# A graph network on one core: who makes the decay weights, who prunes and sums part of each cosine block, and how column sums are turned

## The chip, the cores and the metric

The kernel runs on one core of one Trainium2 chip. The metric is the device time of one execution in microseconds, median of three runs. Engines: TensorE (PE, with its weight loads PEld), VectorE (DVE), ScalarE (ACT), GpSimd (POOL), and SyncE (SP), whose queue issues all loads.

## The reference

The input is x (3327 x 64) and adj (3327 x 3327, about 0.5% non-zero and a full diagonal). Four layers each end in a layer norm of x plus the layer's output.

```python
# layer 0, twice:  x = tanh(concat([adj @ x, x]) @ W[k])
# layer 1:         1 - 0.1 * x - 0.01 * sum(x * (adj @ x), axis=1)
# layer 2:         support = x @ weight; mask = adj != 0; rank = cumsum(mask, axis=1)
#                  w = mask * (pos > 0) * 0.5 ** (k - pos)     # the last 100 neighbours
#                  w @ support + bias
# layer 3, for it in range(2), H = adj:
Q = x @ Wq + bq;  V = x @ Wv + bv;  edge_feat = H.T @ V
att = softmax(Q @ edge_feat.T * scale * H, axis=1);  att_scores = att.mean(axis=0)
comp_mask = softmax(0.5 * structural + 0.5 * att_scores) >= th_comp
cos = xn @ xn.T                                   # of the masked, normalised rows
edge_scores = softmax(cos * H, axis=1)
H_pruned = H * ((edge_scores >= th_edge) & comp_mask[:, None])
connectivity = H_pruned.sum(axis=1)               # row sums; the column sums are edeg
node_mask = softmax(connectivity * feat_mag) >= th_node, where connected
agg = (H_pruned.T * dv_isqrt) @ (x_final @ W) / edeg
x = relu(dv_isqrt * (H_pruned @ agg) @ Theta)
```

## The kernel before

adj is padded to 3328 x 3328 and cut into 26 blocks of 128 rows (1664 KB each in float32). Each stage streams the blocks again; SyncE issues their loads in order, each after a wait for the slot that it overwrites (`block_done`).

The stages, with their times in the profile: two hops and the ODE layer (to 279 us), the decay layer (to about 473), and then twice edge, attention, cosine, down and up (edge 474 to 553, attention 554 to 677, cosine 688 to 900, down and up 904 to 1108; the second iteration ends the kernel).

The decay layer makes, for 26 blocks in two column halves (q = 0, 1), 52 steps. In each, TensorE counts neighbours in PSUM with triangular matrices (`own_bits`, `rest_tri`), ScalarE (`L1015`) and VectorE (`L1270`) turn the counts of two partition halves into bf16 weights with a relu into int16, one half each, in chunks of 512 and 320 columns, and TensorE multiplies them with the support, which was split in three bf16 parts (`split_part`, L1201, starting with a scaling by 2**27, L1206). VectorE also makes the next block's mask (L1254). In the first steps the layer norm of the ODE layer is still under way: it is done in three parts of the nodes (2, then 1, then 0), with `drift_part` (L1191), `centre_part` (L1143), `square_part` and `root_part` on ScalarE, `var_part`, `scale_part`, and then TensorE's turn of x (`early_turn`, L664) and `support_part` (L671). Their places in both queues are written out by step number.

The attention and cosine passes are alike: TensorE makes a block of products in four pieces of 832 columns, VectorE multiplies each with adj and takes the row maximum (`product_piece`, L1317), then the maximum over the pieces (L1328); ScalarE takes the exponential in place with its row sum (L1069). In the cosine pass VectorE then makes the row's cut (`cut_of`, L1439); ScalarE writes the sign of cut minus exponential for the later stages (L1087) and VectorE prunes the block in its slot in one instruction with its row sum (`prune`, L1447), one block behind the pieces. Two product buffers (`prod`) are used in turn. TensorE adds up the columns of the pruned slot two blocks behind (`columns`, L766), which frees the slot; there are four slots.

After each of these passes a row of column sums is copied to SBUF and turned into node order by TensorE (`turn_sums`, L811), in the attention pass ahead of the node softmax, in the cosine pass among the down stage's first blocks. A node softmax has its maximum and sum over partitions on GpSimd (L528, L530), which has nothing else to do after its memsets. `keep_running` puts matmuls with zeros (512 columns) into TensorE's queue.

In down and up the slots are pruned by the stored signs (L1475, L1489) before TensorE gathers.

## Time and profile before

| | |
|---|---|
| median of 3 runs | 1776.97 us (1773.96 to 1777.36) |
| the profiled execution | 1778.09 us, its span 1776.3 us |
| mean granted TensorE clock | 0.954 |
| TensorE busy | 1536.9 us, 87% |
| VectorE busy | 1192.9 us, 67% |
| ScalarE busy | 683.8 us, 38% |
| GpSimd busy | 4.0 us, 17 instructions |
| chain that ended last | PE 50%, DVE 26%, DMA 20%, ACT 2% |
| HBM over the span | 325 GB/s |

The span is what the profiler sees of one execution; the device time is 1.8 us more. Shares are means over all stages. The chain is followed back from the last instruction, at each step to what released it.

### The profile page before, as it was taken

Reading aid. Unit: us, or ns where it says so; the run is one execution under the profiler, and the core shown is the slowest. Engines: PE = TensorE matmul, PEld = TensorE weight load, DVE = VectorE, ACT = ScalarE, POOL = GpSimd, SP = SyncE. Lnnn points to the kernel's source line nnn. Section 1 sums busy time; section 2 is a strip of 40 time slices with the busy share of each in tenths; the row PEclk is TensorE's granted clock in tenths of the full one; section 3 lists DMA queues with packets and bytes.
Section 4 is the critical chain, followed back from the end, with each engine's and each line's share of the span. In section 5 each row is a group of like instructions: output and inputs, shape, how many; then the busy total and the mean of one; then the engine's idle time right before and its main releaser. Section 6 shows DMA issues by size and latency. Waiting matters only on the chain.

```text
span 1776.3 us, 22361 instructions
## 1 busy us (share of the span) xinstructions
PE 1536.9 (87%) x9521; PEld 617.7 (35%) x9549; DVE 1192.9 (67%) x1668; ACT 683.8 (38%) x520; POOL 4.0 (0%) x17
## 2 busy tenths in 40 slices
PE   6789998899999997777787799999997777797895
PEld 2234433334433333222232344443333222232442
DVE  0000306777505996999989798117977999989897
ACT  0000101333213665787720242015665777700441
POOL 0000000000000000000000000000000000000000
PEclk9999999999999999888889999999998888799998
DMA  9979596799799993656579999999992566599993
GB/s 404 427 283 426 231 426 233 245 341 410 304 426 392 394 378 123 221 206 228 193 297 427 420 421 425 426 426 406 381 370 77 196 228 219 179 389 425 426 426 166
DMA packets 60611, 578.29 MB, mean 326 GB/s; under 512 B 6240, under 2 KB 6496, under 8 KB 20832
## 3 DMA queue, kind: packets, MB, share of 16 engines
q1 hardware_dynamic: 60512, 576.87, 81.1%
q8 instruction: 75, 1.23, 0.3%
q14 instruction: 24, 0.20, 0.0%
HBM read 575.14 MB, written 1.70 MB: 325 GB/s over the span
## 4 chain that ended last, share of the span: by engine, by line
PE 50%; DVE 26%; DMA 20%; ACT 2%; issue 2%; SPq 0%; DVEq 0%; POOL 0%; ACTq 0%
PE ps L545 48%; DMA slot<-adj 10%; DVE pairs L1317 10%; DMA arena<-adj_t 7%; DVE slot L1447 7%; DVE slot L1475 3%; DMA slot<-adj_t 2%; PE ps L895 2%; DMA x_kept<-cur 1%; DVE slot L1489 1%; ACT pairs L1069 1%; DVE pairs L1270 1%; DVE hats L1489 0%; DVE hats L1475 0%; DVE pairs L1475 0%
## 5 line engine op out<-in xcount | busy, mean ns | idle before, releaser
L1317 DVE CUSTOM_DVE_ANT_1 pairs<-ps,slot 128x832 f32<-128x832 f32 x352 | 342.6, 1020 | 30.1 <-PE ps L545 14.9
L1069 ACT ACTIVATE pairs<-pairs,negmax 128x3327 f32<-128x3327 f32 x88 | 270.0, 3069 | 135.1 <-DVE negmax L1328 135.1
L545 PE MATMUL ps<-hats 64*128 64x416 f32 x832 | 225.8, 651 | 101.9 <-DVE max L1317 100.7
L545 PE MATMUL ps<-slot,cur 128*64 128x512 f32 (+1 forms) x1536 | 281.1, 515 | 28.7 <-DVE slot L1475 16.2
L545 PE MATMUL ps<-arena 64*128 64x416 f32 (+1 forms) x1072 | 207.6, 524 | 2.2 <-DVE max L1317 1.6
L1447 DVE SCALAR_TENSOR_TENSOR slot<-pairs,cut,slot 128x3327 f32<-128x3327 f32 x52 | 191.1, 3676 | 0.1
L545 PEld LDWEIGHTS ps<-slot,cur 128*64 128x64 f32 x1536 | 103.4, 137 | 202.3 <-issue 163.3
L1087 ACT ACTIVATE arena<-pairs,cut 128x3328 fp8e4<-128x3328 f32 x52 | 159.7, 3072 | 26.3 <-DVE cut L1439 26.3
L545 PEld LDWEIGHTS ps<-hats 64*128 64x128 f32 x832 | 77.8, 216 | 241.1 <-DVE max L1317 194.5
L1137 DVE COPY pairs<-ps 128x512 f32<-128x512 f32 x3 | 2.1, 692 | 195.0 <-PE ps L545 195.0
L545 PEld LDWEIGHTS ps<-arena 64*128 64x128 f32 (+1 forms) x1072 | 87.6, 175 | 122.4 <-DVE max L1317 64.1
L1106 ACT ACTIVATE hats<-ps 128x2048 int16<-128x2048 int16 (+1 forms) x28 | 42.1, 1554 | 227.0 <-PE ps L895 226.9
L545 PE MATMUL ps<-slot,ones 128*32 128x416 f32 x832 | 100.3, 608 | 7.1 <-DVE slot L1447 7.1
L1475 DVE SCALAR_TENSOR_TENSOR slot<-arena,slot 128x3328 f32<-128x3328 int8 x28 | 100.7, 3622 | 6.0 <-DMA slot<-adj 5.9
L545 PE MATMUL ps<-pairs,arena 128*64 128x512 bf16 (+2 forms) x736 | 94.8, 372 | 1.0 <-DMA pairs<-adj 1.0
L545 PE MATMUL ps<-pairs,hats 128*128 128x512 bf16 (+1 forms) x392 | 86.0, 339 | 9.3 <-DVE pairs L1270 6.1
L545 PE MATMUL ps<-slot,arena 128*64 128x512 f32 x480 | 87.8, 515 | 3.3 <-DMA slot<-adj 3.3
L1015 ACT ACTIVATE pairs<-ps 128x512 int16<-128x512 f32 x104 | 53.0, 517 | 92.5 <-PE ps L545 88.2
L1270 DVE TENSOR_SCALAR pairs<-ps 128x512 int16<-128x512 f32 x104 | 60.6, 590 | 37.4 <-PE ps L545 33.1
L948 ACT ACTIVATE pairs<-ps 128x640 f32<-128x640 f32 (+1 forms) x6 | 3.9, 650 | 198.4 <-PE ps L545 198.4
L1489 DVE SCALAR_TENSOR_TENSOR slot<-hats,slot 128x3328 f32<-128x3328 int8 x20 | 72.0, 3620 | 8.6 <-ACT hats L1106 6.4
L545 PE MATMUL ps<-arena,cur 128*64 128x512 f32 (+1 forms) x384 | 68.6, 513 | 1.0 <-DMA arena<-adj_t 1.0
(178 smaller groups left out, 1453.7 us busy)
## 6 DMA issues: line engine op xcount, KB each, us to landing
slot<-adj SPq DMA_DIRECT2D x162, 1664.0 KB, 9.2
slot<-adj_t SPq DMA_DIRECT2D x64, 1664.0 KB, 15.1
arena<-adj_t SPq DMA_DIRECT2D x26, 1664.0 KB, 23.4
arena<-adj_t SPq DMA_DIRECT2D x52, 832.0 KB, 6.5
arena<-adj SPq DMA_DIRECT2D x15, 1664.0 KB, 14.8
pairs<-adj SPq DMA_DIRECT2D x15, 1664.0 KB, 15.6
pairs<-adj_t SPq DMA_DIRECT2D x12, 1664.0 KB, 14.4
hats<-adj SPq DMA_DIRECT2D x8, 1664.0 KB, 12.5
```

The source lines that it names most:

```text
L545: return pe.matmul(o, l, r, start=start, stop=stop, skip_group_check=True)
L895: last = pe.transpose(ps[:, 4 * BANK + q * D:4 * BANK + (q + 1) * D].bitcast(BF16), sign_pairs[:, q * HALF + pair * P:q * HALF + (pair + 1 ...
L948: act.activation(agg_f[:, CHUNK_COLS[c]], ps[:, CHUNK_COLS[c]], ACT.Copy).then_inc(early_cols[c], 1)
L1015: act.activation(dst, bank(c, w), ACT.Relu).then_inc(relu_act, 1)
L1069: act.activation(bufs[b][:, 0:N], bufs[b][:, 0:N], ACT.Exp, bias=negmax[:, b:b + 1], accum_out=rowsum[:, b:b + 1]).then_inc(exp_done, 1)
L1087: act.activation(interleaved(sign_marks[:, row * NP:(row + 1) * NP]), halves(prod[k % 2][:, 0:NP]), ACT.Sign, bias=cut[:, k % 2:k % 2 + 1] ...
L1106: act.activation(turned[pair % 2][:, cols], ps[:, 4 * BANK:4 * BANK + HALF].bitcast(I16)[:, cols], ACT.Copy)\
L1270: dve.tensor_scalar(dst, bank(2 + c, w), 0.0, None, ALU.max).then_inc(relu_dve, 1)
L1317: dve.tensor_tensor_reduce(out=pieces3(bufs[k % len(bufs)], c), in0=pieces_psum(piece_place(name, k, c)[0]), in1=pieces3(slot_of(name, k), ...
L1447: dve.scalar_tensor_tensor(out=slot[:, 0:N], in0=prod[k % 2][:, 0:N], scalar=cut[:, k % 2:k % 2 + 1], in1=slot[:, 0:N], op0=ALU.is_ge, op1 ...
L1475: dve.scalar_tensor_tensor(out=slot, in0=interleaved(signs[:, row * NP:(row + 1) * NP]), scalar=0.0, in1=slot, op0=ALU.is_le, op1=ALU.mult ...
L1489: dve.scalar_tensor_tensor(out=slot, in0=interleaved(turned[k // 2 % 2].bitcast(I8))[:, k % 2], scalar=0.0, in1=slot, op0=ALU.is_le, op1=A ...
```

## The change

In the decay layer ScalarE makes both halves' weights in the first ten steps (`ACT_STEPS`). The weight of the support is scaled by 2**27 once at the start, and the split reads PSUM itself. A part's drift is centred through its row sums: a reduce over the whole of `scr_a` is done ahead, the mean then follows from small operations. Part 1's drift comes behind the split of part 2, ScalarE's square, turn and copy of the parts move by a step.

After an attention pass eight fillers stand ahead of the last block's column sums and three instead of six behind; eight instead of twelve follow the turn. The turn is thirteen transposes and a matmul into two banks; VectorE reads the result with four instructions instead of one.

In the cosine passes the last 512 columns of blocks 0 to 23 are pruned by GpSimd (a comparison into `share_marks`, then a product in the slot), and summed by ScalarE, which copies them into `share_sink` with a row sum, one block behind, after the next block's exponential and sign. VectorE prunes the other columns and adds the sums of both. The column sums, the reuse of `prod` and the slots' reloads wait for the new steps. Behind its last share GpSimd makes a reduction of ones over the partitions that nobody reads.

```diff
+ACT_STEPS = 10
+def weights_made(q, k, c):
+    n = 2 * (q * NB + k) + c + 1
+    return n + min(n, 2 * ACT_STEPS), max(0, n - 2 * ACT_STEPS)
...
+SHARE = 512
+SHARED = NB - 2
...
+        def turned_sums(t):
+            at = 4 * BANK + t * P if t < MID else 6 * BANK + (t - MID) * P if t < 2 * MID else 4 * BANK + MID * P
+            return ps[:, at:at + P]
...
+                    behind = free - 1 - BASE[f"cos{it}"]
+                    if kind in ("cos", "down") and 0 <= behind < SHARED:
+                        sp.wait_ge(share_summed, it * SHARED + behind + 1)
...
+            def prune_share(it, k):
+                slot = slot_of(f"cos{it}", k)
+                cols = slice(N - SHARE, N)
+                pool.wait_ge(row_cut, it * NB + k + 1)
+                if it * SHARED + k:
+                    pool.wait_ge(share_pruned, it * SHARED + k)
+                pool.tensor_scalar(share_marks[:, :], prod[k % 2][:, cols], cut[:, k % 2:k % 2 + 1], None, ALU.is_ge)\
+                    .then_inc(share_marked, 1)
+                pool.wait_ge(share_marked, it * SHARED + k + 1)
+                pool.tensor_tensor(slot[:, cols], slot[:, cols], share_marks[:, :], ALU.mult).then_inc(share_pruned, 1)
...
             for it in range(2):
                 node_softmax(2 * it)
+                for k in range(SHARED):
+                    prune_share(it, k)
+                pool.partition_all_reduce(tiny["unused"][:, :], ones32[:, 0:1], P, RADD).then_inc(reduction_loaded, 1)
                 node_softmax(2 * it + 1)
...
+            pe.wait_ge(consts_made, 5)
+            pe.wait_ge(consts_cast, 4)
             support_part(2)
-            pe.wait_ge(consts_made, 5)
-            pe.wait_ge(consts_cast, 3)
             for q in range(2):
                 if q:
-                    pe.wait_ge(relu_act, 2 * NB)
-                    pe.wait_ge(relu_dve, 2 * NB)
+                    by_act, by_dve = weights_made(0, NB - 1, 1)
+                    pe.wait_ge(relu_act, by_act)
+                    pe.wait_ge(relu_dve, by_dve)
...
-                        pe.wait_ge(relu_act, 2 * (q * NB + k) + c + 1)
-                        pe.wait_ge(relu_dve, 2 * (q * NB + k) + c + 1)
+                        by_act, by_dve = weights_made(q, k, c)
+                        pe.wait_ge(relu_act, by_act)
+                        if by_dve:
+                            pe.wait_ge(relu_dve, by_dve)
...
+                        if k < SHARED:
+                            pe.wait_ge(share_pruned, it * SHARED + k + 1)
...
                 columns(NB - 2)
+                pe.wait_ge(piece_read, (g + 1) * NB * 4 + 5)
+                keep_running(8 if sums else 0)
                 columns(NB - 1)
-                pe.wait_ge(piece_read, (g + 1) * NB * 4 + 5)
                 mm(bank(5, 1), zeros_b[:, :], ones_b[:, 0:1]).then_inc(colsum_psum, 1)
-                keep_running(6)
+                keep_running(3 if sums else 6)
...
-                whole, split = ident[:, 0:P:D], ident[:, 32:P:D]
-                for t in range(MID):
-                    mm(turned_sums[:, 2 * t:2 * t + 2], col_rows[:, t * P:(t + 1) * P], whole)
-                    b = MID + 1 + t
-                    mm(turned_sums[:, 2 * b:2 * b + 2], col_rows[:, D + t * P:D + (t + 1) * P], split)
-                middle = turned_sums[:, 2 * MID:2 * MID + 2]
-                mm(middle[0:D], col_rows[:, MID * P:MID * P + D], whole)
-                mm(middle[D:P], col_rows[:, 0:D], split).then_inc(colsum_t, 1)
+                for t in range(2 * MID):
+                    o = t * P + t // MID * (P // 2 - MID * P)
+                    pe.transpose(turned_sums(t), col_rows[:, o:o + P], ident)
+                pe.transpose(turned_sums(2 * MID)[0:D], col_rows[:, MID * P:MID * P + D], ident)
+                mm(turned_sums(2 * MID)[D:P], col_rows[:, 0:D], ident).then_inc(colsum_t, 1)
...
-                keep_running(12)
+                keep_running(8)
...
-            square_part(4, 1)
...
+                        if q * NB + k < ACT_STEPS:
+                            act.wait_ge(tri_done, 4 * (q * NB + k) + 2 * c + 2)
+                            dst = decay[k % 2].bitcast(I16)[:, QUART + o:QUART + o + w]
+                            act.activation(dst, bank(2 + c, w), ACT.Relu).then_inc(relu_act, 1)
                     if q == 0 and k == 0:
+                        square_part(4, 1)
                         root_part(4, 1)
-                    elif q == 0 and k == 1:
+                    elif q == 0 and k == 2:
                         early_xt(1)
-                    elif q == 0 and k == 2:
                         square_part(5, 0)
                     elif q == 0 and k == 4:
                         root_part(5, 0)
-                    elif q == 0 and k == 5:
+                    elif q == 0 and k == 6:
...
+                def sum_share(k):
+                    at = place(ROW_ORDER["cos"][k])
+                    act.wait_ge(share_pruned, it * SHARED + k + 1)
+                    if it * SHARED + k:
+                        act.wait_ge(share_summed, it * SHARED + k)
+                    act.activation(share_sink[:, :], slot_of(f"cos{it}", k)[:, N - SHARE:N], ACT.Copy,
+                                   accum_out=small["conn_share"][:, at:at + 1]).then_inc(share_summed, 1)
                 for k in range(NB):
                     exp_and_sign(k)
+                    if 0 < k <= SHARED:
+                        sum_share(k - 1)
...
+            def drift_product(c):
+                dve.wait_ge(folded, 6 + 3 - c)
+                link(dve.tensor_tensor(of_part(scr_b, c), blocks3(early_psum(c)), of_part(cur[:, :], c), ALU.mult))
             def drift_part(c):
-                dve.wait_ge(folded, 6 + 3 - c)
                 mean = part_small(small["mean"][:, :], c)
-                link(dve.tensor_tensor(of_part(scr_b, c), blocks3(early_psum(c)), of_part(cur[:, :], c), ALU.mult))
                 link(dve.tensor_reduce(mean, of_part(scr_b, c), axis=X, op=ALU.add))
-                link(dve.tensor_scalar(mean, mean, 0.01, None, ALU.mult))
-                link(dve.tensor_tensor(of_part(scr_a, c), of_part(scr_a, c), part_spread(small["mean"][:, :], c),
-                                       ALU.subtract))
+                drift = part_small(small["dv"][:, :], c)
+                link(dve.tensor_scalar(drift, mean, 0.01, None, ALU.mult))
+                link(dve.scalar_tensor_tensor(out=mean, in0=part_small(small["rnorm"][:, :], c), scalar=1.0 / D, in1=drift,
+                                              op0=ALU.mult, op1=ALU.subtract))
+                link(dve.tensor_tensor(mean, mean, drift, ALU.add))
+                dve.tensor_tensor(of_part(scr_a, c), of_part(scr_a, c), part_spread(small["mean"][:, :], c),
+                                  ALU.subtract).then_inc(part_centred, 1)
...
-                link(dve.tensor_scalar(part, blocks3(early_psum(c)), float(1 << DECAY_SHIFT), None, ALU.mult))
-                link(dve.tensor_copy(sup[:, :, 0], part))
-                link(dve.tensor_tensor(part, part, sup[:, :, 0], ALU.subtract))
+                link(dve.tensor_copy(sup[:, :, 0], blocks3(early_psum(c))))
+                link(dve.tensor_tensor(part, blocks3(early_psum(c)), sup[:, :, 0], ALU.subtract))
...
+            dve.tensor_scalar(W["decay_w"], W["decay_w"], float(1 << DECAY_SHIFT), None, ALU.mult).then_inc(consts_cast, 1)
...
+            link(dve.tensor_reduce(small["rnorm"][:, :], blocks3(scr_a), axis=X, op=ALU.add))
             early_evac(2, "ode")
+            drift_product(2)
             drift_part(2)
-            centre_part(2)
-            drift_part(1)
+            drift_product(1)
             var_part(3, 2)
             ready_part(3, 2)
-            centre_part(1)
...
             split_part(2)
+            drift_part(1)
             for q in range(2):
                 if q:
                     mask_of(0, q)
                     mask_of(1, q)
                 for k in range(NB):
-                    dve.wait_ge(decay_used, q * NB + k + 3)
-                    for c, (o, w) in enumerate(QUART_CHUNKS):
+                    for c, (o, w) in enumerate(QUART_CHUNKS if q * NB + k >= ACT_STEPS else ()):
+                        if c == 0:
+                            dve.wait_ge(decay_used, q * NB + k + 3)
...
+                        drift_product(0)
                         drift_part(0)
-                    elif q == 0 and k == 2:
-                        centre_part(0)
...
+                            dve.wait_ge(share_marked, g // 2 * SHARED + min(k - 1, SHARED))
...
+            def on_column_sums(g, use):
+                dve.wait_ge(colsum_t, g + 1)
+                def pairs_of(t, part, rows):
+                    v = t[rows, 2 * part * (MID + 1):2 * part * (MID + 1) + 2 * MID]
+                    return v.rearrange("p (b h) -> p b h", h=2)
+                everything = slice(0, P)
+                for part in range(2):
+                    v = ps[:, (4 + 2 * part) * BANK:(4 + 2 * part) * BANK + MID * P]
+                    v = v.rearrange("p (b h r z) -> p b h r z", h=2, r=2, z=32)[:, :, :, part, 0]
+                    use(v, lambda t, part=part: pairs_of(t, part, everything))
+                    rows = slice(part * D, part * D + D)
+                    v = turned_sums(2 * MID)[rows].rearrange("p (h r z) -> p h r z", h=2, r=2)[:, :, part, 0]
+                    last = use(v, lambda t, rows=rows: t[rows, 2 * MID:2 * MID + 2])
+                return last
...
-                dve.wait_ge(colsum_t, 2 * it + 1)
-                link(dve.scalar_tensor_tensor(out=S["node_z"], in0=turned_sums, scalar=0.5 / N, in1=S["imp"],
-                                              op0=ALU.mult, op1=ALU.add))
+                def score(sums, of):
+                    return dve.scalar_tensor_tensor(out=of(S["node_z"]), in0=sums, scalar=0.5 / N, in1=of(S["imp"]),
+                                                    op0=ALU.mult, op1=ALU.add)
+                link(on_column_sums(2 * it, score))
...
-                    dve.scalar_tensor_tensor(out=slot[:, 0:N], in0=prod[k % 2][:, 0:N],
-                                             scalar=cut[:, k % 2:k % 2 + 1], in1=slot[:, 0:N], op0=ALU.is_ge,
+                    cols = slice(0, N - SHARE if k < SHARED else N)
+                    dve.scalar_tensor_tensor(out=slot[:, cols], in0=prod[k % 2][:, cols],
+                                             scalar=cut[:, k % 2:k % 2 + 1], in1=slot[:, cols], op0=ALU.is_ge,
                                              op1=ALU.mult, accum_out=S["conn"][:, at:at + 1]).then_inc(pruned, 1)
...
+                dve.wait_ge(share_summed, (it + 1) * SHARED)
+                link(dve.tensor_tensor(S["conn"], S["conn"], S["conn_share"], ALU.add))
...
-                        dve.wait_ge(colsum_t, 2 * it + 2)
-                        dve.tensor_scalar(S["edeg"], turned_sums, 1e-6, None, ALU.max).then_inc(edeg_read, 1)
+                        on_column_sums(2 * it + 1, lambda sums, of: dve.tensor_scalar(
+                            of(S["edeg"]), sums, 1e-6, None, ALU.max)).then_inc(edeg_read, 1)
```

## Rows read from the trace of the kernel before

**Rows 1.** Windows: length; busy PE, PEld, DVE, ACT, POOL; PE clock, DMA share, GB/s.
```profile
440.00:450.00 10.00, 9.84 (x67) 3.82 (x68) 7.50 (x11) 3.60 (x7) 0.00 (x0) 1.00 1.02 412
450.00:460.00 10.00, 9.84 (x71) 3.94 (x70) 6.02 (x10) 3.52 (x8) 0.00 (x0) 1.00 0.24 91
680.00:900.00 220.00, 163.47 (x888) 55.28 (x891) 203.99 (x322) 162.36 (x80) 0.74 (x2) 0.85 0.50 180
900.00:1000.00 100.00, 85.36 (x492) 33.48 (x490) 83.73 (x37) 5.93 (x8) 0.74 (x2) 0.98 0.97 403
```

**Rows 2.** Timeline of a cosine block: start, duration, instruction, [idle before].
```profile
714.37 0.16 DVE L1328 TENSOR_REDUCE negmax<-max 128x1 f32<-128x4 f32 x1
714.45 3.67 DVE L1447 SCALAR_TENSOR_TENSOR slot<-pairs,cut,slot 128x3327 f32<-128x3327 f32 x1
717.54 0.19 ACT L1069 ACTIVATION_READ_ACCUMULATOR pairs<-pairs,negmax 128x1 f32 x1
718.05 0.15 DVE L1439 SCALAR_TENSOR_TENSOR cut<-rowsum,blocked 128x1 f32<-128x1 f32 x1
718.37 1.02 DVE L1317 CUSTOM_DVE_ANT_1 pairs<-ps,slot 128x832 f32<-128x832 f32 x1 [0.17 <-DVE slot L1447]
722.27 0.16 DVE L1328 TENSOR_REDUCE negmax<-max 128x1 f32<-128x4 f32 x1
722.46 3.07 ACT L1069 ACTIVATE pairs<-pairs,negmax 128x3327 f32<-128x3327 f32 x1 [1.15 <-DVE negmax L1328]
```

**Rows 3.** Timeline where the cut of block 1 waits for the exponential.
```profile
702.09 0.19 ACT L1069 ACTIVATION_READ_ACCUMULATOR pairs<-pairs,negmax 128x1 f32 x1
702.31 0.16 DVE L1439 SCALAR_TENSOR_TENSOR cut<-rowsum,blocked 128x1 f32<-128x1 f32 x1 [2.46 <-ACT pairs L1069]
```

**Rows 4.** Timeline of GpSimd's memset at the start and its first reduction.
```profile
0.86 0.53 POOL L520 MEMSET ones_b<- 128x512 bf16 x1
...
683.06 0.18 DVE L1357 TENSOR_REDUCE pmax<-node_z 128x1 f32<-128x26 f32 x1
683.33 0.35 POOL L528 PARTITION_ALL_REDUCE gmax<-pmax  x1 [681.71 <-DVE pmax L1357]
```

**Rows 5.** First cosine pass: waits (total, times, longest), and the chain (start, length).
```profile
DVE pairs L1317 <- DMA slot<-adj: 3.9, 4, 1.9
...
814.38 8.65 DMA slot<-adj
```

**Rows 6.** Timeline of the decay stage's start; last, its row of waits.
```profile
279.99 0.82 DVE L1195 TENSOR_TENSOR arena<-ps,cur 128x640 f32<-128x640 f32 x1 [0.79 <-PE ps L660]
286.94 0.82 DVE L1152 TENSOR_REDUCE mean<-arena 128x10 f32<-128x640 f32 x1
289.26 1.33 PE L668 MATMUL ps<-cst,cur 128*128 128x128 f32 x5 [3.26 <-DVE cur L1159]
294.46 0.83 DVE L1206 TENSOR_SCALAR arena<-ps 128x640 f32<-128x640 f32 x1 [1.86 <-PE ps L545]
...
298.81 1.02 PE L545 MATMUL ps<-pairs,hats 128*128 128x512 bf16 x4
334.73 1.04 PE L545 MATMUL ps<-pairs,hats 128*128 128x512 bf16 x4
337.64 1.04 PE L545 MATMUL ps<-pairs,hats 128*128 128x512 bf16 x4
...
PE ps L545 <- DVE pairs L1270: 6.1, 15, 1.0
```

**Rows 7.** Groups by form, 300 to 400 us: ScalarE's weights of a decay step.
```profile
L1015 ACT ACTIVATE pairs<-ps 128x512 int16<-128x512 f32 x31 | 18.5, 595 | 29.9 <-PE ps L545 27.8 <-remote 2.1
L1015 ACT ACTIVATE pairs<-ps 128x320 int16<-128x320 f32 x31 | 13.5, 437 | 21.0 <-PE ps L545 21.0
```

**Rows 8.** Timeline: turning the column sums, and thirteen transposes elsewhere.
```profile
679.84 2.95 PE L545 MATMUL ps<-cst,pairs 128*128 128x2 f32 x28
...
279.18 1.64 PE L660 MATMUL ps<-cst,pairs 128*128 128x128 f32 x13
```

12 lines of the change are left out of this document (9 added, 3 removed).

## The prediction

> **What bounds the kernel now.** I read busy time by stage first, then the chain that ended last, then the instructions in order of time where the change touches them. TensorE's share over the whole span misleads, as the stages differ [rows 1]. In the decay stage (300 to 450 us) TensorE is the limit: busy 9.84 of 10 us. In the down stage the DMA queues are full, at 403 GB/s, and up and the next edge stage are like it. In the cosine pass (680 to 900, and a second one like it in iteration 1) VectorE is busy 204 of 220 us, DMA half the time, and TensorE waits, at a mean clock of 0.85. A gain in a cosine pass is kept, since the DMA-bound stretch behind it starts when the pass is over; a gain inside a DMA-bound stretch is lost.
>
> The cosine pass in order of time [rows 2]. Per block VectorE does four pieces (P), the maximum (M), the pruning of the block before (R, 3.67) and the cut (C); ScalarE does the exponential (E), then the sign (S). From M at 714.37: R, then C at 718.05 (3.68 later), P at 718.37, next M at 722.27: a period of 7.90 us. E, its accumulator read included, is over at 717.73, M+3.36. R is the later of the two, but only by 0.3 us. ScalarE idles 1.15 us ahead of the next E, so S ended at M+6.94.
>
> **The cosine prune.** R loses 512 of 3327 columns: at 3.67/3327 per column 0.57 us. C then waits for E instead. How fast C follows E is shown where it waits for it already: E's accumulator read ends at 702.28, C starts at 702.31 [rows 3]. So C comes at M+3.39 instead of M+3.68, and the period becomes 7.61: of 0.57 us 0.29 is paid out. It counts for blocks 2 to 24, 23 per pass, since C(1) waits for E already and R of the last two blocks stays whole: 6.7 us per pass.
>
> ScalarE gets a copy of 512 columns with a sum. Nearest rows: an activation of 128x512 in the decay stage, 0.595 [rows 7], and 0.19 for the read of an accumulator [rows 2]: 0.8 us, between S(k) and E(k+1). S would end at M+6.65, the copy at M+7.45, E(k+1) may start at M+7.80. It fits, with some 0.35 us left. A copy of over 1.15 us would begin to eat the gain; at 1.45 it is gone. Slot reloads now wait for this sum too, but the column sums of the same block on TensorE end after M(k+2), and this sum before it, so that costs nothing.
>
> GpSimd gets two operations of 512 columns per block, from C(k) on. The trace shows none of the kind. Nearest row: its memset of 128x512, 0.53 [rows 4], one stream. A stream for each operand read and for the result makes 2 + 3 of them, 2.65 us: my value. Two memsets, 1.1 us, are the low end, twice the value, 5.3 us, the high end. VectorE's next R starts 4.2 us after C (0.32 to P, 3.90 to M). Up to there GpSimd runs beside the pieces and costs nothing; nor does TensorE wait, as the sums of block k come two blocks later. The Trainium skill speaks against the change here: SBUF — State Buffer, section Who interferes with whom, has it that a VectorE instruction with two SBUF inputs and a GpSimd instruction that reads SBUF shut each other out, the later one waiting in full. R has two such inputs, a piece one (the other is PSUM); no run here shows it yet, and by that rule R suffers only if GpSimd's pair outlasts the gap. GPSIMD Engine Reference, section Instruction dispatch, gives about 2.5 cycles per element for two inputs, an estimate of 1.1 us for the second operation; the sum would be the same.
>
> GpSimd's reductions over partitions may need code that the prune displaces. Before, the first of them starts 0.09 us after what it waits for [rows 4], so any loading was hidden there. The unused sum stands behind GpSimd's last share, some 17 us before the node softmax wants the engine, which hides it. At the first share the slack is two C apart, 6.4 us from C(0) to the P(2) that waits for its mark. I put nothing down, and 2 us per pass as the bad end.
>
> Against this stands the reload of slots. Block k+4 waits for the column sums of block k. In the first cosine pass four pieces waited for DMA, 3.9 us in all [rows 5]: one block's sums ended at 814.38, the load took 8.65 us, and that was up to 1.9 too long. Sums come late where the granted clock is at its lower level, 1.2 GHz; I take some eight to ten of the 26 in a pass. With the shorter period each has 2 x 0.29 = 0.58 us less slack, and most have little. I take 2.5 us per pass back (bounds 0, and 5.8 for ten). Net per pass 4.2, both 8.4. One addition of 26 columns joins the chain at each pass's end, 0.2 us as another of that width takes 0.18 [rows 4]: minus 0.4.
>
> **The start of the decay stage** [rows 6]. VectorE begins the drift of part 2 at 279.99 and has it centred at 284.66; then it does part 1's drift before it comes to the variance at 286.94; TensorE's transposes of the new x start at 289.26, the split of the support at 294.46, step 0 at 298.81. After: the second reduce and one subtract go (0.85 each with its gap), one small operation of 0.2 comes: centred at 283.2. Only part 1's product (0.7) stands ahead of the variance, which ScalarE's square lets start at 284.0: 3.0 us earlier, and the transposes too, at 286.3. The split loses its first operation of 0.83 and reads PSUM twice instead, 3.6 down to 3.0. Step 0 starts near 295.2, 3.6 us earlier. The new full reduce stands where VectorE waits for the last gathers; it costs nothing.
>
> Steps 0 to 9: step 9 starts at 334.73, 35.9 us after step 0. TensorE's own pace is 2.91 (the next step starts at 337.64), nine times 26.2; two turns and two support parts among them take 3.6. So 6.1 us are waits, mostly for VectorE's share of the weights, which queues behind its layer-norm work: 6.1 us in 15 waits from 300 to 470 us [rows 6]. After, ScalarE makes all of them: two of 512 and two of 320 columns, at 0.595 and 0.437 [rows 7], 2.1 us of the 2.91. The pair that gates the next step takes 1.2 of the 2.1 us that TensorE needs from its release. I walked the ten steps: one wait stays, about 2 us ahead of step 1, because ScalarE's root of part 1 stands ahead of its weights and needs VectorE's variance at 298.2. Step 1 then starts at 299.6, step 5 at 313.0, step 9 at 326.5: 8.2 us earlier. Is it kept? DMA is full up to 450, yet TensorE is busy 9.84 of 10 us there, and then DMA idles (0.24 in 450 to 460) until slots are free [rows 1]: it follows the steps, and moves with them. I count all 8.2; 5 is the low end, with one more wait of ScalarE's.
>
> **The end of an attention pass.** Turning the sums takes 28 instructions, 2.95 us [rows 8]; thirteen transposes take 1.64 [rows 8], the one matmul left two of the 28, 0.2. The start moves up 0.3, as six fillers become three. VectorE then has four operations for one: 0.5 more. Gain 0.9 to 1.1; 1.1 us, twice: 2.2. The eight fillers ahead of the last sums go into TensorE's idle time there; at the low clock they would cost up to 1.5. The same turn in the down stage gains nothing, as the queues are full [rows 1]. The scaled weight, the waits for constants and a memset lie at the start beside DMA: nothing.
>
> **Sum.** 8.2 + 2.2 + 8.4 - 0.4 = 18.4 us. The profiled execution took 1778.1 (span 1776.3); minus 18.4 is 1759.7. It lies 1.1 above the runs' median, 1777.0, so the median after is 1758.6; I say 1759.
>
> **Rivals.**
> First: GpSimd runs into R and, where both want the same path to SBUF, R waits. Place: every prune. With a pair of length p, C to C is p+3.44 (0.05 to start, R 3.15 and its read 0.08, C 0.16). That equals 7.61 at p = 4.17 and 7.90 at 4.46; the other parts bring 10.0, so the whole breaks even at p = 4.68 and is slower from there: at p = 5.3, 46 x 0.84 - 10.0 = 29 us slower, 1806. Were the pieces held off too by a pair of 2.65, 46 x 2.4 - 10.0 makes 100 us slower. For it: 1.1 to 5.3 is a wide range and the gap is 4.2. Against: my value of 2.65. The rule on the shared path is this rival's. Chance 0.12.
> Second: the cosine pass gives nothing, because loads take it all or ScalarE's copy is over 1.4 us: 8.2 + 2.2 - 0.4 = 10.0, 1767. For: margins of 0.35 and 0.58. Against: only a third of the sums is late. Chance 0.20.
> Third: the decay steps give little, because ScalarE, now alone, is late: its queue holds two squares and two roots in those steps, each waiting for VectorE. 3 us instead of 8.2: 1764. Against: 0.8 us free per step. Chance 0.13.
> Fourth: the change doesn't do what it says: GpSimd needs new code within each share and can't keep up, several us per block, far over 1800. Its kinds of operation alternate only twice per pass; 0.02.
>
> **Numbers.** The forecast has 0.53. A measurement tells about 0.2%, 3.5 us, from no change. Faster 0.84, same 0.03, slower 0.13. The range runs from 1751 (the full 6.7 per pass, and 3 more at the front) to 1771 (the second rival with 5 at the front); the first and the fourth, and a little, are outside.
>
> **What would show it.** C waits for E, about 0.1 us per block, with a period of 7.6; GpSimd's pair lies between C and M; ScalarE idles some 0.3 us ahead of E; the waits of pieces for DMA grow from 3.9 us in pass 0; step 9 starts near 326.5. I am wrong if R is longer than 3.2, if anything in the pass waits for GpSimd, or if step 9 starts after 330.

## The result, and the profile after

The changed kernel takes 1749.31 us (median of 4, 1748.2 to 1750.99) where the kernel before took 1777.16 beside it: a ratio of 0.985 [0.983, 0.987]. Run again beside later runs of the kernel before it came to 1746.47, ratio 0.983 [0.981, 0.984]. The gain is 27 to 31 us by the two ratios; 18.4 were forecast, and 1749.3 lies 1.7 us below the forecast's range. The profiled span went from 1776.3 to 1748.8 us.

The page after, its head and the chain of waits:

```profile
span 1748.8 us, 22672 instructions
...
PE 1527.7 (87%) x9499; PEld 612.5 (35%) x9499; DVE 1159.4 (66%) x1659; ACT 721.7 (41%) x636; POOL 138.0 (8%) x115
...
PE 51%; DMA 22%; DVE 18%; ACT 7%; issue 2%; SPq 0%; DVEq 0%; POOL 0%; ACTq 0%; POOLq 0%
```

VectorE lost 33 us of work, ScalarE gained 38 and GpSimd 134. DVE's share of the chain fell from 26 to 18%, ACT's rose from 2 to 7%.

Windows of the changed kernel (each line a stretch of time with the busy time of each engine; columns as in [rows 1]):

```profile
440.00:450.00 10.00, 9.86 (x72) 4.05 (x72) 5.78 (x9) 3.54 (x7) 0.00 (x0) 1.00 0.18 71
450.00:460.00 10.00, 10.00 (x67) 4.46 (x63) 6.40 (x11) 1.10 (x2) 0.00 (x0) 1.00 0.80 301
680.00:900.00 220.00, 169.74 (x896) 55.30 (x896) 197.80 (x321) 179.26 (x131) 67.74 (x51) 0.84 0.56 201
```

The idle DMA that stood at 450 to 460 us [rows 1] now stands at 440 to 450: the loads follow TensorE's steps and moved with them.

A cosine block after, timeline (start, duration, instruction, [idle before]; answers to [rows 2]; VectorE, then ScalarE, then GpSimd):

```profile
713.71 0.16 DVE L1524 SCALAR_TENSOR_TENSOR cut<-rowsum,blocked 128x1 f32<-128x1 f32 x1 [0.16 <-ACT pairs L1113]
713.95 1.02 DVE L1383 CUSTOM_DVE_ANT_1 pairs<-ps,slot 128x832 f32<-128x832 f32 x1
...
717.85 0.16 DVE L1394 TENSOR_REDUCE negmax<-max 128x1 f32<-128x4 f32 x1
717.92 3.14 DVE L1533 SCALAR_TENSOR_TENSOR slot<-pairs,cut,slot 128x2815 f32<-128x2815 f32 x1
...
721.24 0.16 DVE L1524 SCALAR_TENSOR_TENSOR cut<-rowsum,blocked 128x1 f32<-128x1 f32 x1 [0.16 <-ACT pairs L1113]
...
716.88 0.61 ACT L1140 ACTIVATE share_sink<-slot 128x512 bf16<-128x512 f32 x1
717.40 0.19 ACT L1140 ACTIVATION_READ_ACCUMULATOR share_sink<-slot 128x1 f32 x1
718.04 3.07 ACT L1113 ACTIVATE pairs<-pairs,negmax 128x3327 f32<-128x3327 f32 x1 [0.46 <-DVE negmax L1394]
...
713.97 1.56 POOL L556 TENSOR_SCALAR share_marks<-pairs,cut 128x512 bf16<-128x512 f32 x1 [4.80 <-DVE cut L1524]
715.61 1.09 POOL L559 TENSOR_TENSOR slot<-slot,share_marks 128x512 f32<-128x512 f32 x1
```

From cut to cut it is 7.53 us. R takes 3.14, the cut waits 0.16 for ScalarE's exponential, GpSimd's pair lies from 713.97 to 716.70, 1.2 us ahead of the next R, and ScalarE still idles 0.46.

The start of the decay stage after (answers to [rows 6]):

```profile
286.98 0.77 PE L708 MATMUL ps<-cst,cur 128*128 128x128 f32 x5 [0.33 <-DVE cur L1213]
...
288.63 1.35 PE L585 MATMUL ps<-hats,arena 128*128 128x128 f32 x10
...
298.00 1.02 PE L585 MATMUL ps<-pairs,hats 128*128 128x512 bf16 x4 [1.43 <-ACT pairs L1059]
...
324.23 1.04 PE L585 MATMUL ps<-pairs,hats 128*128 128x512 bf16 x4
```

Step 9 starts at 324.23, 10.5 us earlier than at 334.73. The five transposes take 0.77 us, where before they took 1.33 behind an idle time of 3.26 [rows 6]. Windows of that stretch, the kernel before:

```profile
288.00:291.00 3.00, 1.74 (x7) 1.36 (x8) 2.77 (x6) 0.47 (x2) 0.00 (x0) 0.54 0.00 0
291.00:294.00 3.00, 3.00 (x13) 2.40 (x11) 1.60 (x2) 0.84 (x2) 0.00 (x0) 0.50 0.28 54
```

and after:

```profile
288.00:291.00 3.00, 2.98 (x19) 1.90 (x18) 1.74 (x3) 0.48 (x1) 0.00 (x0) 1.00 0.52 152
```

The granted clock was 0.54 and 0.50, near and at the level of 1.2 GHz, and is 1.00, the level of 2.4.

### The profile page after: what moved, and what is told of

The parts are those of the page before. It is cut to its first block, busy times and chain, and to the rows that moved or that the text cites. A ratio compares the mean times of both kernels' runs of the same rounds, so it can differ in the third digit from the quotient of the medians.

```text
span 1748.8 us, 22672 instructions
## 1 busy us (share of the span) xinstructions
PE 1527.7 (87%) x9499; PEld 612.5 (35%) x9499; DVE 1159.4 (66%) x1659; ACT 721.7 (41%) x636; POOL 138.0 (8%) x115
## 4 chain that ended last, share of the span: by engine, by line
PE 51%; DMA 22%; DVE 18%; ACT 7%; issue 2%; SPq 0%; DVEq 0%; POOL 0%; ACTq 0%; POOLq 0%
PE ps L585 48%; DMA slot<-adj 12%; DVE pairs L1383 9%; DMA arena<-adj_t 9%; ACT pairs L1113 5%; DVE slot L1562 3%; PE ps L936 2%; DMA slot<-adj_t 2%; DVE slot L1576 1%; DVE slot L1533 0%; DVE hats L1576 0%; DVE pairs L1562 0%; DVE hats L1562 0%; ACT arena L1131 0%; ACT hats L1160 0%
## 5 line engine op out<-in xcount | busy, mean ns | idle before, releaser
L585 PE MATMUL ps<-hats 64*128 64x416 f32 x832 | 220.9, 640 | 93.5 <-DVE max L1383 92.2
L1533 DVE SCALAR_TENSOR_TENSOR slot<-pairs,cut,slot 128x2815 f32<-128x2815 f32 (+1 forms) x52 | 165.5, 3183 | 0.1
L556 POOL TENSOR_SCALAR share_marks<-pairs,cut 128x512 bf16<-128x512 f32 x48 | 80.9, 1685 | 243.4 <-DVE cut L1524 243.4
## 6 DMA issues: line engine op xcount, KB each, us to landing
pairs<-adj_t SPq DMA_DIRECT2D x12, 1664.0 KB, 14.4
```

Of the source, the lines that this page charges most:

```text
L556: pool.tensor_scalar(share_marks[:, :], prod[k % 2][:, cols], cut[:, k % 2:k % 2 + 1], None, ALU.is_ge)\
L585: return pe.matmul(o, l, r, start=start, stop=stop, skip_group_check=True)
L1533: dve.scalar_tensor_tensor(out=slot[:, cols], in0=prod[k % 2][:, cols], scalar=cut[:, k % 2:k % 2 + 1], in1=slot[:, cols], op0=ALU.is_ge, ...
```

## The experiments

Fourteen runs. I read each trace at six events: the last exponential of the first attention pass, the first and last sign of each cosine pass, the last exponential of the second attention pass. The stages between them are the front (up to the first event), the two ends of the attention passes (from an attention pass's last exponential to the first sign) and the two cosine passes (from first to last sign). The table says by how many us each stage was shorter than in the one trace of the kernel before:

```
                             front  end 1  pass 1  end 2  pass 2
changed                        9.8    1.4     6.3    4.5     5.8
changed, again (e6)           11.8    1.4     6.1    4.5     7.6
e1 without the share          10.2    1.4     3.3    4.5     1.7
e2 without the decay part      0.9    1.4     6.4    4.5     6.1
e3 without the new turn       12.2    0.0    10.2    1.5     7.6
e4 ACT_STEPS = 0               5.5    1.4     9.3    4.5     6.9
e5 before, 12 more fillers     0.3    0.0     2.7    3.1     1.2
e7 share of 1024              10.1    1.4     9.0    4.5     6.2
e8 share of 256                9.2    1.4     8.1    4.5     6.6
e9 fillers in the passes      10.7    1.4    11.3    4.5     9.2
e10 and in more places        11.6    1.4    12.3    4.5     9.7
e11 no first fillers          12.0    0.0     9.2    3.0     7.3
e12 no unused sum             10.6    1.4     5.8    4.5     6.0
e13 e9 without the share      11.3    1.4     2.6    4.5     1.2
e14 before, fillers as in e9   0.6   -1.7     3.2    1.4     1.4
```

Between the last sign of pass 1 and the last exponential of the second attention pass nothing moved by more than 0.8, but for e5, which lost 3.8 there. A "filler" is one of the idle multiplications of zeros. The trace of the kernel before is one of several: e2's front gives 0.9 and e14's 0.6 with the old code, so numbers against a single trace are uncertain by about that much there, and by some us in the passes. Where a run is set against the changed kernel by medians, I use the mean of its two ratios, 0.9838.

**Undoing one part.** e1 prunes all columns on VectorE:

```diff
-                    cols = slice(0, N - SHARE if k < SHARED else N)
+                    cols = slice(0, N)
```

(with GpSimd's and ScalarE's share, the unused sum and the addition to the row sums gone).

> The changed kernel with the cosine part undone: VectorE prunes all 3327 columns of every block again, no share for GpSimd and ScalarE, no unused sum, no addition of 26 columns. Everything else as changed. Theory: the cosine share is worth what the two traces show between the last attention exponential's end and the last R of each pass, 6.3 and 5.7 us, so the run comes at 1749.3 + 12 = 1761 us, the cosine period goes back to 7.90 and C waits for R. Rival (the sizes of the forecast were right, and the rest came from elsewhere): it loses only 8.0, 1757. Rival two (the pass gains nothing and both stretches are shifted by clock): 1750 to 1752.

Measured 1757.21 us, ratio 0.990 [0.989, 0.992]: 11 us slower than the changed kernel by the ratios. The period is 7.89 again. But the passes were still 3.3 and 1.7 us shorter than before, with the same code: its pieces waited 0.3 us a pass for loads, not 3.9 and 2.1. So these waits are not a property of the code alone, and a difference of two traces misprices a pass by some us.

e2 puts back the old drift, centring, split and the weights of the first ten steps:

```diff
-ACT_STEPS = 10
...
+                link(dve.tensor_scalar(part, blocks3(early_psum(c)), float(1 << DECAY_SHIFT), None, ALU.mult))
```

> The changed kernel with the decay part undone: drift, centring, split of the support and the first ten steps' weights as before (half on VectorE, half on ScalarE). The cosine share and the new turn of the column sums stay. Theory: step 9 goes back by about 10.4 us (324.2 to 334.7) and the whole by as much, 1759 to 1760; the first transposes of the new state come at the lower clock again (L668 in 1.3 rather than 0.8 us per group), and the support products take about 2.3 instead of 1.35. Rival: the clock in that stretch has nothing to do with the edit and stays high: the loss is the forecast's 8.2, 1757.5.

Measured 1758.56 us, 0.991 [0.988, 0.993]: 12 us slower, the front gone but for 0.9. The clock's part of my theory held by halves: the support products took 2.34 us, but the transposes ahead of them still 0.77, behind the same idle time as before:

```profile
289.68 0.77 PE L699 MATMUL ps<-cst,cur 128*128 128x128 f32 x5 [3.26 <-DVE cur L1198]
```

e3 puts back 28 instructions for the turn, six fillers behind the sums and twelve behind the turn, none ahead:

```diff
-                keep_running(8 if sums else 0)
...
-                keep_running(8)
+                keep_running(12)
```

> The changed kernel with the end of an attention pass as before: column sums turned by 28 small instructions, no eight fillers ahead of the last sums, six instead of three fillers behind them, and twelve instead of eight behind the turn. Theory: both ends lose what the traces show, 1.4 and 4.5 us, of which about 3 us are the lower clock that TensorE had at the end of the second pass before: 1755. Rival: the clock at the second end is a matter of where the stretch falls in time and not of these instructions; the loss is the forecast's 2 x 1.1 us, 1751.5.

Measured 1748.84 us, 0.985 [0.984, 0.987]: 2 us by the ratios, within what two runs differ by, and neither theory's time. The stages tell more. The first end lost its 1.4 us, as expected; the second kept 1.5 of 4.5, where the theory had 0 and the rival 3.4. Passes and front happened to be shorter by more than that. What the second end lost is in the fillers behind the turn: twelve of them took 4.33 us there and 2.76 at the first end.

e4:

```diff
-ACT_STEPS = 10
+ACT_STEPS = 0
```

> The changed kernel with one constant changed: in the first ten decay steps VectorE and ScalarE halve the weights again, instead of ScalarE making all. The reordered drift, the shorter split and all else stay. Theory: step 0 stays at 293.6, but steps 0 to 9 take again some of the waits that left (35.9 us from step 0 to step 9 before, 30.6 after): 5 us of loss, 1754. Rival: those waits came from the old place of part 0's drift and centring (moved too) and not from who makes the weights: 1749 to 1750.

Measured 1753.46 us, 0.988 [0.986, 0.989]; the front fell to 5.5 of a mean of 10.9 over the eleven traces that hold the whole decay part. The weights' move to ScalarE is half of the front, as the theory had it and the rival had not. But step 0 didn't stay where it was: VectorE makes its half of the first weights only behind part 1's drift, and step 0 starts some 2 us later for it (295.23 for 293.59, though the transposes began 0.5 earlier), with TensorE at the low level:

```profile
295.23 1.86 PE L585 MATMUL ps<-pairs,hats 128*128 128x512 bf16 x4 [2.02 <-DVE pairs L1336]
```

**The clock at the decay start.** e5 changes the kernel before in one number:

```diff
-            keep_running(24)
+            keep_running(36)
```

> The kernel before with one number changed: 36 instead of 24 idle multiplications of zeros behind the transposes at the end of the Euler steps (L662), so that TensorE is busy until the new state comes at 289.26 instead of idling 3.26 us. Theory (clock): TensorE is then still at its high level in the next 5 us; the five transposes take 0.77 instead of 1.33, the four fillers 1.03 instead of 1.91, ten support products 1.35 instead of 2.3, and step 0 starts at about 296.5 instead of 298.8; the run 1775.6 - 2 = 1773.5. Rival (the stretch is set by VectorE and ScalarE, the clock only fills waits): step 0 at 298.5 or later, no change.

Timeline of TensorE in e5:

```profile
280.73 7.93 PE L545 MATMUL ps<-ones_b,zeros_b 128*128 128x512 bf16 x36
289.34 0.77 PE L668 MATMUL ps<-cst,cur 128*128 128x128 f32 x5 [0.67 <-DVE cur L1159]
...
296.94 1.02 PE L545 MATMUL ps<-pairs,hats 128*128 128x512 bf16 x4
```

VectorE delivers at the same time (289.34 for 289.26), but TensorE had idled only 0.67 us, and step 0 starts at 296.94 instead of 298.81. From the transposes to step 0 it is 7.60 us, against 9.55 in the kernel before, and 8.57 and 8.45 in e2 and e14, which have the same code and the same idle time of 3.26 there: the clock is worth 0.9 to 1.9 us at this place. The median is 1772.33, ratio 0.998 [0.996, 0.999], 4 us faster. In this trace the 1.9 were held to the end of the decay stage (the turn at 470.45 for 472.30) and all but 0.2 lost in the next 25 us, where the granted clock was 0.91 (windows 470 to 490) for 1.00 before. So where the 4 us of the median come from is not shown.

**The changed kernel again** (e6), as a control:

> The changed kernel once more, as the control of the runs that undo one part. After four of these, undoing the cosine share cost 9, the decay part 10 and the turn of the sums nothing by the medians, 20 together, where the whole gained 27. Theory (the rest is scatter in the DMA-bound stretches and in the loads of the cosine pass): the same starts up to 300 us to within 0.1, the attention ends again give 1.4 and 4.5, and what varies is how long pieces wait for DMA in the cosine passes, between 1 and 6 us per pass; the median within 3 us of 1749. Rival (a real interaction between the parts): the passes repeat at 5.5 and 3.7 us of DMA waits.

1746.47 us, within the theory's 3. The waits for loads in the passes were 5.6 and 1.3 us, for 5.5 and 3.7: the rival holds for one pass, not for the other. That the starts agree to within 0.1 up to 300 us was wrong: the transposes at 286.98 came at 286.37, as the Euler steps had ended 0.6 earlier. Over the seven traces with the share at 512 columns and the clock as granted the passes gained 11.8 to 17.8 us together, 14.4 on the mean; over the three without share and fillers 0, 5.0 and 3.9. The difference, 11.4, agrees with the 11 us of e1, though single traces of either kind differ by 5 to 6 us.

**The size of the share.** e7 and e8:

```diff
-SHARE = 512
+SHARE = 1024
```

> The changed kernel with a share of 1024 instead of 512 columns for GpSimd and ScalarE. GpSimd's pair was 1.56 + 1.09 for 512; for 1024 it takes about 5.3 with its gap, more than the 4.2 us between C and R. Theory A (VectorE's prune and GpSimd's operations shut each other out, as the first share shows, 4.52 us beside a running prune instead of 1.56): R can't start until the second operation is over, it starts late or is drawn out by 1.1 us or more, R itself, 2303 columns, needs 2.55 + 0.08 us; C follows at about p + 2.9 from C, so the period is near 8.2 to 8.4 and the run 46 x 0.75 = 35 us slower than the changed kernel, 1784, if the loads don't hide it. Theory B (no such lock): R of 2.6 us is over long before E, ScalarE needs 3.07 + 3.27 + 1.4 = 7.7 us per block, and becomes the bound; the period is near 7.75, 10 us slower than the changed one, 1759.

Timeline of a block in e7:

```profile
699.49 0.15 DVE L1524 SCALAR_TENSOR_TENSOR cut<-rowsum,blocked 128x1 f32<-128x1 f32 x1
...
699.74 2.84 POOL L556 TENSOR_SCALAR share_marks<-pairs,cut 128x1024 bf16<-128x1024 f32 x1 [2.59 <-DVE cut L1524]
...
702.66 1.99 POOL L559 TENSOR_TENSOR slot<-slot,share_marks 128x1024 f32<-128x1024 f32 x1
...
703.76 3.31 DVE L1533 SCALAR_TENSOR_TENSOR slot<-pairs,cut,slot 128x2303 f32<-128x2303 f32 x1
...
707.08 0.16 DVE L1524 SCALAR_TENSOR_TENSOR cut<-rowsum,blocked 128x1 f32<-128x1 f32 x1
```

Measured 1748.85 us, 0.984 [0.982, 0.986]: the same as at 512 within the measurement, so both theories failed as to the time. The mechanism of A is there all the same. R has 2303 columns, 2.54 us at 3.67/3327; it took 3.31, and the 0.8 more is the time in which GpSimd's second operation still ran (to 704.65). Where I went wrong is the price: the pair is 4.92 and not 5.3, and R is 0.6 shorter than at 512, which pays for the hold. The cuts come 7.59 apart here and 7.58 on the median, for 7.53 at 512.

e8 (`SHARE = 256`):

> The changed kernel with a share of 256 instead of 512 columns. R then takes 3.43 instead of 3.14 us and ends at M+3.46 with its gap, 0.1 after E's accumulator read at M+3.36. Theory: VectorE becomes the later one again by 0.1, the period goes from 7.53 to about 7.65; 23 x 0.12 x 2 = 5 us slower before the loads take part back, 1752 to 1754. Rival (only that E is later than R counts, at either size nearly the same): 1750, as C waits for E in both.

VectorE in e8:

```profile
706.89 0.15 DVE L1524 SCALAR_TENSOR_TENSOR cut<-rowsum,blocked 128x1 f32<-128x1 f32 x1
707.19 1.02 DVE L1383 CUSTOM_DVE_ANT_1 pairs<-ps,slot 128x832 f32<-128x832 f32 x1
...
714.50 0.16 DVE L1524 SCALAR_TENSOR_TENSOR cut<-rowsum,blocked 128x1 f32<-128x1 f32 x1
```

Measured 1749.18 us, 0.984 [0.983, 0.986]. The period is 7.61, as the forecast had it for 512 columns, and the piece follows the cut by 0.30 where it does by 0.24 at 512. With R of full width it is 0.32 [rows 2]. So some of the piece's delay falls away once R is over well before the cut; that it is R's own completion for which the piece waits is how I read it, not shown. The 0.08 x 46 = 3.7 us that this is worth can't be seen in the median. One reason is on record: the pieces of both passes waited 2.4 us for loads in e8 and 2.2 in e7, and 5.9 on the mean of the seven traces at 512 (2.8 to 9.2). So equal times don't show that the three sizes are equal; the periods, 7.58, 7.53 and 7.61, put 512 ahead by 2 to 4 us.

**Fillers in the cosine passes.** e9 adds zeros to the bank of the column sums:

```diff
                     for k in range(2, NB):
+                        keep_adding_zero(5)
                         piece(k, 3)
                         if k + 1 < NB:
+                            keep_adding_zero(2)
                             piece(k + 1, 0)
```

where each is `mm(bank(6), zeros_b[:, :], ones_b[:, :], start=False)`.

> The changed kernel with idle multiplications in the cosine passes: in each block from the third on, TensorE adds five products of zeros of 512 columns to the bank of the column sums ahead of piece 3 and two ahead of the next block's piece 0, where it waited about 2.2 and 1.3 us for VectorE. Theory (the low clock of the cosine pass, 0.85 granted, makes column sums late, and late sums make slot loads late): the granted clock of 700 to 860 us goes to 0.97 or more, TensorE's share from 78% to some 85%, and the waits of pieces for DMA, 5.5 and 3.7 us in one run and 5.6 and 1.3 in another, fall below 1 per pass: 4 to 8 us faster than the changed kernel, about 1742. Rival (the loads' own length sets these waits, not the clock of the sums): no change, 1748. Rival two (the clock stays at its low level, and seven fillers of 0.43 us each overrun the idle time): each block later by 0.5 us, 1765.

Windows of e9:

```profile
700.00:860.00 160.00, 146.63 (x832) 46.52 (x830) 152.88 (x254) 144.27 (x106) 56.30 (x43) 1.00 0.64 229
```

The same window of the changed kernel, and its wait for loads in pass 1:

```profile
700.00:860.00 160.00, 124.89 (x658) 40.06 (x660) 150.57 (x248) 141.72 (x104) 54.58 (x42) 0.85 0.62 224
...
DVE pairs L1383 <- DMA slot<-adj: 5.5, 5, 1.8
```

The granted clock went from 0.85 to 1.00, and among the waits of both passes no row of a piece waiting for a load is left. Measured 1743.03 us, 0.982 [0.981, 0.984]; that is 3 us below the changed kernel by the ratios, where the intervals overlap, but each of its four times lies below each of the eight of e11 and e12, taken beside it. The median load from 700 to 860 us took 6.9 us, in the changed kernel 7.2, hardly more. The sixteen column sums of a block, which free its slot, took 1.60 us at most up to 872 us; in the changed kernel eight rows of them took 1.70 to 2.90. The theory holds, with a gain at or below the low end of its 4 to 8 us.

e10 adds fillers ahead of the last cosine sums and of the two turns at the end of the decay stage:

```diff
-                keep_running(8 if sums else 0)
+                keep_running(8)
...
+                        keep_high(6)
                         turn_part(0, 1, cur)
+                        keep_high(3)
                         turn_part(0, 2, cur)
```

> The one before it, and two more places with idle multiplications: eight ahead of a cosine pass's last column sums (3.00 us at the low clock, 1.60 at the high one), and six and three ahead of the two turns of the new state at the end of the decay stage (idle 1.27 and 0.62 us; behind them 32 products took 7.50 us in the run with a share of 256 and 5.81 in the repeat of the changed kernel). Theory (clock): 1 us at the first pass's end and one at the second's, and 0.8 on the mean at the end of the decay stage: 2 to 3 us below the one before. Rival (the gather behind is bound by its loads, so nothing ahead of it counts): the same as the one before.

Timeline of TensorE at the end of pass 1 in e10:

```profile
873.16 2.67 PE L585 MATMUL ps<-ones_b,zeros_b 128*128 128x512 bf16 x8
875.76 1.60 PE L585 MATMUL ps<-slot,ones 128*32 128x416 f32 x16
...
879.17 11.18 PE L585 MATMUL ps<-slot,cur 128*64 128x512 f32 x60 [0.38 <-DVE cur L1570]
```

Measured 1740.25 us, 0.980 [0.979, 0.982], the fastest of all, 2.0% below the kernel before's 1774.69 beside it. The last sums take 1.60 instead of 3.00, and the gather now waits 0.38 for VectorE, so there is no more to be had at this place. The step from e9 to e10, 2.8 us, is as expected, but the two intervals overlap.

**Without the first fillers** (e11):

```diff
-                keep_running(8 if sums else 0)
```

> The changed kernel without the eight idle multiplications ahead of the last column sums of an attention pass. Theory (they keep the clock up over the end of the pass, where the traces show 3.0 us more gained at the second end than with the old turn): the turn of the sums at the second end runs at the low clock again, about 2 us slower there, the first end 0.5 to 1: 1750. Rival (the fewer instructions of the turn make the 3.0 us): the ends stay at 1.4 and 4.5, 1748.

TensorE at the second end, e11:

```profile
1306.70 2.59 PE L585 MATMUL ps<-pairs,row_rz 128*1 128x416 f32 x16 [2.02 <-DVE row_rz L1490]
...
1310.50 1.49 PE L859 MATMUL ps<-cst,pairs 128*128 128x128 f32 x12
```

and in the changed kernel:

```profile
1308.00 1.90 PE L585 MATMUL ps<-ones_b,zeros_b 128*128 128x512 bf16 x8
1309.99 1.58 PE L585 MATMUL ps<-pairs,row_rz 128*1 128x416 f32 x16
```

Measured 1747.46 us, 0.985 [0.983, 0.986]: too little for a median, but the stages are plain: 0.0 and 3.0 instead of 1.4 and 4.5. Without the eight fillers the changed kernel loses 1.5 us at each end, as the sums take 2.6 and not 1.58. My reason was half right: the turn behind them runs at the high clock either way (1.49). But the fillers only hold what the kernel before had: there the same sums took 1.58 us too, at both ends of all four traces with the old turn, behind 1.93 us of idle time. Why 2.02 us of it in e11 brought the low level and 1.93 there did not, no run shows.

What the new end gains over the old one lies behind the sums. In the kernel before, second end, the node mask (`comp_b`) is made from 1335.71 on, but TensorE begins the work that waits for it only at 1338.84, behind its twelve fillers:

```profile
1333.61 5.30 PE L545 MATMUL ps<-ones_b,zeros_b 128*128 128x512 bf16 x12
1338.84 1.24 PE L545 MATMUL ps<-ident_b,comp_b 128*64 128x128 bf16 x26
...
1335.71 0.24 DVE L1366 TENSOR_SCALAR comp_b<-node_e,gsum 128x26 bf16<-128x26 f32 x1 [0.96 <-POOL gsum L530]
```

In the changed kernel the eight fillers take 1.90 us and are over before the mask:

```profile
1316.97 0.92 PE L585 MATMUL ps<-ident_b,comp_b 128*64 128x128 bf16 x26 [0.78 <-DVE comp_b L1450]
```

**Without the unused sum** (e12): one line less on GpSimd.

> The changed kernel without the unused sum over partitions. Both theories agree that some loading of code lies ahead of the next reduction, the trace shows GpSimd idle 7.9 us ahead of the unused one with nothing to wait for. Theory: it is paid in the open at the end of both cosine passes, since GpSimd then waits with it for the row maximum: 2 x 6 to 8 us slower, about 1762. Rival (the loading goes on while the engine waits, as it does ahead of the attention pass): no change, 1748.

GpSimd in the changed kernel, and in e12:

```profile
871.76 0.40 POOL L573 PARTITION_ALL_REDUCE unused<-ones  x1 [7.90 <-issue]
883.26 0.37 POOL L564 PARTITION_ALL_REDUCE gmax<-pmax  x1 [11.10 <-DVE pmax L1441]
```

```profile
882.97 0.38 POOL L564 PARTITION_ALL_REDUCE gmax<-pmax  x1 [17.24 <-DVE pmax L1440]
```

Measured 1746.75 us, 0.984 [0.982, 0.986]: no loss. The maximum that it waits for is ready at 882.83 (its start 882.65 and 0.18), the reduction starts 0.14 later, and nothing of the 7.9 us shows. At the second pass it is the same (0.14 behind a wait of 17.81). The rival holds: whatever fills that time goes on while the engine waits. The unused sum does nothing for this kernel.

**The share with the clock up.** e13 is e9 without the share (edit as in e1).

> The idle multiplications of the cosine pass kept (five and two of 512 columns per block), the cosine share taken out: VectorE prunes all columns. Beside the same kernel with the share (1743.0) it prices the share with the waits for loads gone on both sides. Theory (with the clock up nothing is taken back): the period is 7.90 against 7.53, 46 blocks x 0.37 = 17 us, less 0.4 for the addition: 1759 to 1760. Rival (the share is worth what undoing it cost without the fillers, 9 to 11 us): 1753.

Measured 1757.41 us, 0.989 [0.988, 0.990], 12 us above e9 by the ratios, 14 by the medians, 14.6 by the spans. In the passes it is 20.5 against 3.8, 16.7 us, and the period is 7.89 against 7.53. So the theory's 17 holds in the passes of the traces, while the times lie between it and the rival's 9 to 11; in the trace some 2 us of it come back in stretches that the edit does not touch.

e14 puts e9's fillers into the kernel before.

> The kernel before with the same idle multiplications in its cosine passes and nothing else. Theory (late loads follow from the low clock in the kernel before too): the waits for DMA of the passes, 3.9 and 2.1 us in its trace, go to under 0.5, the granted clock of 700 to 860 us from 0.85 to 1.00: 4 to 6 us faster, 1770. Rival (at a period of 7.90 the loads have slack enough and the waits were chance): 0 to 2 us, 1774.

Windows of e14:

```profile
700.00:860.00 160.00, 137.96 (x764) 44.05 (x767) 152.82 (x241) 126.18 (x62) 0.00 (x0) 0.97 0.57 203
```

Measured 1771.13 us, 0.996 [0.995, 0.998], 6 us faster, and no wait of a piece for a load is left in either pass. So the kernel before lost time to this too. How much is not settled: its passes gained 4.6 us, but those of e5, without these fillers, 3.9.

## Why the prediction was wrong in size

The direction held, and so did the mechanisms that the sum named. Three terms were too small, one of them because a part of the edit stood in no term.

**The start of the decay stage**: forecast 8.2, measured 10.9 on the mean of eleven traces (9.2 to 12.2), or 10.4 against the mean of the three with the old code there (before, e2, e14). Step 0 came 5.2 us earlier, not 3.6 (4.8 on the means), and steps 0 to 9 gave 5.3, not 4.6. The single wait that I had left, ahead of step 1 for ScalarE, is there: 1.43 us, for 2. What failed is the step to "Step 0 starts near 295.2": I moved TensorE's work at its old durations, 1.33 for five transposes, and 2.34 for the ten support products, though that was the low level after 3.26 us of idle time, which the change closes. From the transposes (forecast 286.3, measured 286.98) to step 0 the forecast has 8.9 us, the changed kernel 6.61; e5, e2 and e14 put 0.9 to 1.9 of it down to the clock.

**The ends of the attention passes**: forecast 1.1 each, measured 1.4 and 4.5 against the trace of before, 1.9 and 3.0 against the mean of four traces with the old turn (before, e3, e5, e14), 4.9 us where I had 2.2. The gain that I worked out is there: the maximum that follows the turned sums starts 1.13 us earlier, counted from the last exponential. The "up to 1.5" that the eight fillers would cost did not come; they keep the sums at 1.58. What failed is a term that I left at nothing: the fillers behind the turn, twelve before and eight now. The old twelve ran on until the work behind them was late, by 0.3 us at the high level, where they took 2.76 us, and by 1.9 to 2.9 us at the low one, where they took 4.33 to 5.3. The new eight take 1.90 and end before the mask is ready, so that the new end has the same length, 21.33 us, in every trace that has it whole, and the old one 22.75 to 25.86. This is read from 32 ends in the traces; no run changed the fillers behind the turn alone.

**The cosine share**: forecast 13.4 gross, 5.0 taken back, 8.4 net. The gross sum is 17 by the period, 7.90 to 7.53, which is 0.37, not 0.29, times 46 (e13: 16.7 in the passes). The step that failed is that the piece would follow the cut by 0.32 as before; it does by 0.24. What the loads take back has the cause that I gave, sums at the low level, but its size is not settled. By the passes it is 4.9: with the clock up they gained 20.5 (e9; e10 has 22.0), with it as granted 14.4 (6.1 lost); without the share 4.2 (mean of e13 and e14) and 3.0 (1.2 lost). By the rows of pieces that wait for loads it is 3.2 (5.9 on the mean of the seven traces with the share, 2.7 on that of the three without). By the ratios the share is worth 12 us with the clock up and 11 as granted, which leaves 1, with an uncertainty as large as the whole term. So my 5.0 may be right by luck. Net it is 11.4 by the passes and 11 by e1's ratio.

10.4 + 4.9 + 11.4 - 0.4 is 26.3 us; the ratios say 27 and 31, 29 on the mean. The 1 to 4 us that are left are within what the front and the passes differ by from trace to trace; where they come from is not shown. The last term held: the addition takes 0.18 us at the end of a pass.

**The rivals.** The second (nothing from the passes) fell: ScalarE's copy takes 0.61 and its read 0.19, the 0.8 that I had. The third fell with e4. The fourth fell: GpSimd's two operations lie 0.08 us apart. The first fell at this size, as the pair takes 2.74 (I had 2.65) of the 4.2 us to R. But its path is real. The first share of each pass starts beside a running R:

```profile
684.92 3.15 DVE L1533 SCALAR_TENSOR_TENSOR slot<-pairs,cut,slot 128x2815 f32<-128x2815 f32 x1
...
685.00 4.52 POOL L556 TENSOR_SCALAR share_marks<-pairs,cut 128x512 bf16<-128x512 f32 x1 [11.15 <-DVE cut L1524]
```

R was started first and ran its 3.15 us; GpSimd took 4.52 instead of 1.56, the 3.0 more being R's rest. In e7 the order is the other way about, and R was held 0.8 us. Pieces, which read one operand from PSUM, took 1.02 us beside GpSimd as ever. The Trainium skill's rule (SBUF — State Buffer, section Who interferes with whom), that the later of the two waits in full where both use the shared port, and that an instruction of VectorE with one input from SBUF isn't concerned, agrees with all three. The estimate of 1.1 us for the second operation, from the Trainium skill's 2.5 cycles per element (GPSIMD Engine Reference, section Instruction dispatch), met 1.09.

**The signs that I named**: the cut waits for E (24 times in pass 1, 6.7 us, of them 3.0 in one), period 7.53 for 7.6, GpSimd's pair between C and M, 0.46 idle for 0.3, waits for loads up from 3.9 to 5.5, step 9 at 324.2 for 326.5. None of the three signs of being wrong appeared, which shows that I had listed none for "too small": a duration at the low clock that becomes one at the high clock.

## What to carry to other kernels

Before moving a TensorE instruction in time, read its duration against the same form elsewhere: where it is nearly double, the clock is part of the edit, and closing the idle time ahead of it may give back the difference (0.9 to 1.9 us here). Harmless multiplications in idle time cost a dozen lines and gave 3 us (e9) and 6 us (e10) beyond the change, by the ratios, of which the first alone is hardly clear of the noise. But they must be over before the operand of the work behind them is ready, and at the low level too: twelve of them, 2.76 us at the high level and up to 5.3 at the low, are what made the old second end late. Where an edit changes the number of such fillers, give them a term of the sum. Where two traces of nearly one kernel differ in waits for loads, take a third before pricing anything by them; price a part by undoing it and by the same stage in every trace at hand, as medians here can't tell 2 us. And when one engine gives work to another, size the share by when the next conflicting instruction starts, and try half and double; here 256, 512 and 1024 columns took the same time within the measurement, and only the periods tell them apart.
